# GpSimd's order of work inside an attention batch: the low halves of the weights move from the front to between the keys and the queries

## The reference

```python
x = x + tanh(g_xattn[0]) * attention(layernorm(x), ctx, ctx)   # 32 query heads, 8 key heads, D = 16, softmax over 128
x = x + tanh(g_ffn[0]) * ffn(layernorm(x))
# ffn: router logits over 7 experts, the 2 highest of each row, softmax over those two;
#      each expert and one shared expert: u = x Wup + b; g = silu(u Wgate + b) * u; g Wdown + b
#      result = sum over the two experts of prob * expert(x)  +  shared(x)
```

## Time and profile before

| | before |
|---|---|
| median of 3 runs | 1243.54 us (1243.29 to 1244.3) |
| the profiled execution's own time | 1242.8 us |
| its span, first to last instruction | 1240.7 us |
| TensorE busy over the span | 1154.8 us (93%) |
| VectorE busy | 818.6 us (66%) |
| ScalarE busy | 535.8 us (43%) |
| GpSimd busy | 388.8 us (31%) |
| the 32 `weights_lo` (L708), mean of one | 99.4 us, 3107 ns |
| mean granted TensorE clock | 0.982 of full speed |

### The profile page before, as it was taken

The page is one execution under the profiler, slowest core; times in us unless marked ns, Lnnn a source line. Parts: engine busy times, 40 slices in busy tenths (PEclk is TensorE's granted clock), DMA queues, the critical chain, the costliest instruction groups (busy, mean ns, idle before and its releaser), DMA issues.

```text
span 1240.7 us, 38694 instructions
## 1 busy us (share of the span) xinstructions
PE 1154.8 (93%) x14378; PEld 844.5 (68%) x14378; DVE 818.6 (66%) x1421; ACT 535.8 (43%) x1082; POOL 388.8 (31%) x454
## 2 busy tenths in 40 slices
PE   3878889999979999989899999999999999999998
PEld 2534444554456777778688887888888888877775
DVE  4888989999979689544444544544444444447898
ACT  2767779989889322122222222222222222222221
POOL 4465766666750000111111111111111110006762
PEclk9988999999979999999999999999999999999999
DMA  5675456565575253586644467435943346249985
GB/s 182 209 261 178 156 171 204 197 201 207 188 255 212 69 129 103 202 224 162 197 124 119 135 202 221 110 104 162 262 116 101 101 126 179 68 142 216 290 261 177
DMA packets 190496, 214.65 MB, mean 173 GB/s; under 512 B 115168, under 2 KB 115680, under 8 KB 190432
## 3 DMA queue, kind: packets, MB, share of 16 engines
q1 hardware_dynamic: 179712, 178.66, 47.9%
q0 software_dynamic: 10720, 35.14, 9.6%
HBM read 324.34 MB, written 64.49 MB: 313 GB/s over the span
## 4 chain that ended last, share of the span: by engine, by line
PE 51%; DVE 14%; SPq 12%; issue 9%; DMA 6%; POOL 3%; ACT 3%; DVEq 1%; ACTq 0%; POOLq 0%
PE PS L1675 29%; PE PS L1716 14%; DVE negm L1023 6%; SPq L459 3%; SPq L424 3%; PE PS L1496 3%; DMA bd<-in_bdown 2%; DMA qB<-negT 2%; PE PS L1530 2%; SPq L386 1%; SPq L420 1%; PE PS L1516 1%; ACT x2n L893 1%; POOL whl L708 1%; DVE xn L1009 1%
## 5 line engine op out<-in xcount | busy, mean ns | idle before, releaser
L1675 PE MATMUL PS<-uhl,wb 128*128 128x128 f16 (+1 forms) x4128 | 280.4, 229 | 8.5 <-DVE uhl L1277 7.9
L1675 PEld LDWEIGHTS PS<-uhl,wb 128*128 128x128 f16 x4128 | 264.9, 98 | 31.1 <-DVE uhl L1277 6.7
L1675 PE MATMUL PS<-xT,wb 128*128 128x128 f16 (+1 forms) x4128 | 279.8, 229 | 4.3 <-DVE gate L1164 1.6
L938 ACT ACTIVATE sl<-PS,bb 128x128 f32<-128x128 f32 (+1 forms) x344 | 106.9, 388 | 406.6 <-PE PS L1675 406.6
L1675 PEld LDWEIGHTS PS<-xT,wb 128*128 128x128 f16 x4128 | 264.0, 98 | 13.5 <-DVE gate L1164 1.7
L1716 PE MATMUL PS<-wb,ghl 128*128 128x512 f16 x1200 | 267.2, 379 | 1.2 <-DVE ghl L1289 1.2
L1716 PEld LDWEIGHTS PS<-wb,ghl 128*128 128x128 f16 x1200 | 115.9, 98 | 131.6 <-DVE ghl L1289 1.5
L928 ACT ACTIVATE u<-PS,bb 128x128 f32<-128x128 f32 (+1 forms) x344 | 106.8, 388 | 197.8 <-PE PS L1675 133.1
L759 POOL COPY ixr<-idx 128x2 int32 (+1 forms) x35 | 8.2, 233 | 549.1 <-DMA xT<-xs 406.7
L1023 DVE TENSOR_REDUCE negm<-PS 128x8 f16<-128x1024 f32 x128 | 155.2, 1212 | 26.2 <-PE PS L1496 25.5
L1284 DVE TENSOR_TENSOR g<-sl,u 128x512 f32<-128x512 f32 x102 | 70.5, 692 | 150.9 <-ACT sl L938 150.8
(11 more groups left out here) (159 smaller groups left out, 1201.4 us busy)
## 6 DMA issues: line engine op xcount, KB each, us to landing
wb<-wsc SPq DMA_DIRECT2D x219, 1024.0 KB
wst<-in_wall SPq DMA_DIRECT2D x32, 768.0 KB, 6.0
wsc<-whl SPq DMA_DIRECT2D x32, 768.0 KB, 4.4
ysl<-yb SPq DMA_DIRECT2D x43, 512.0 KB
bd<-in_bdown SPq DMA_DIRECT2D x74, 256.0 KB
X<-in_x SPq DMA_DIRECT2D x8, 1024.0 KB, 6.5
qB<-qT SPq DMA_DIRECT2D x32, 256.0 KB, 2.9
xnd<-xhl SPq DMA_DIRECT2D x32, 256.0 KB, 2.0
```

Of the source, the lines that this page charges most:

```text
L938: ins = act.activation(sl[:, m, ts], bank_of(PS[1], t, m, kind), ACT.Silu, bias=bb[:, par, bias_slot(kind, t), 1, m:m + 1], scale=1.0 / WS)
L1675: ins = pe.matmul(bank_of(bank, t, m, kind), wb[:, j, l, k, w, m * P:(m + 1) * P], rhs(x, k)[:, ts], start=(n == 0), stop=(n == len(TERMS) ...
```

## The change

In GpSimd's turn the call of `weights_lo` moves from the first place to the place between `split_k` and `split_q`. No operation is added, removed or resized, and no semaphore changes. The other four engines' programs are as they were.

```diff
                 after = follow(half, par, quad, 2)
                 later = follow(half, par, quad, 3)
-                if not start:
-                    weights_lo(*pv)
                 if after is not None:
                     values(*after)
                 if later is not None:
                     split_k(*later[:2])
+                if not start:
+                    weights_lo(*pv)
+                if later is not None:
                     split_q(*later[:2])
```

## The result

| | before | after |
|---|---|---|
| median, 22 runs of each | 1243.92 us (1238.57 to 1252.1) | 1248.28 us (1246.22 to 1252.11) |
| ratio to before | | 1.0031, 95% interval 1.0017 to 1.0045 |
| the profiled execution's own time, its span | 1242.8, 1240.7 us | 1246.86, 1244.8 us |
| mean granted TensorE clock | 0.982 | 0.971 |
| mean of the 32 `weights_lo` (L708) | 3107 ns | 3110 ns |

The change makes the kernel 0.31% slower, 3.9 us (0.0031 x 1243.92; the two medians as they stand differ by 4.4). The prediction was 1243.6 us with a range to 1246.6 and most of its chance on "no change": it was wrong. The changed kernel's lines lie one higher than before from the change on: L1467 is L1468, L1496 is L1497, L1009 is L1010, L1052 is L1053.

What follows compares the result with a forecast made beforehand. TensorE and VectorE were taken to bound attention's loop, with effects only in batches 1 to 12. Terms -0.44, -0.15 and +0.65 gave +0.06 us on 1242.8, 1242.9; plus 0.7 to the runs' median, 1243.6 us, range 1240.0 to 1246.6.

Steps and rivals of the forecast that it cites:

- What bounds the kernel; where the change acts: Attention: TensorE and VectorE busy some 47 of 50 us in the loop; effect only in batches 1 to 12, loop unchanged.
- What is late next: Even batches: VectorE's `xn` ends 0.64 us later, `qx` gets in before `wst`; `wst` and `maxes` come 1.51 us later.
- VectorE goes first: Rival, even batches: `wst` gets the ports before waiting `qx`, together -2.5 us, 1241.0 us; chance 0.17.
- The sum by batches, even turns: Start of `rec` in batches 6, 8, 10: -0.44, -0.15, +0.65 us; batch 2 gives 0; sum +0.06 us.
- The absorbed delays of batches 1, 4 and 12: Delays there taken as 0 behind DMA waits or late high halves; +2.0 us in the sum with their bounds.
- The sum by batches, odd turns: Batches 7, 9 and 11: no term of their own in the sum; the loop and the rest were put at 0.
- TensorE's idle time moves to the maxima products (L1496) behind them: Sign expected in the new profile if right: TensorE idles before these products, released by `maxes`; no cost given.
- where the granted clock is lost: Part of the unseen remainder, with where big transfers fall: both ways by 2 to 3 us; chance 0.10 together.
- The plain sum: Batches 6, 8, 10: three long `kx` waits, 4.9 us, gone; as rival at most 4.3 us, 1239.3 us; chance 0.05.

## Why the prediction was wrong

**What bounds the kernel; where the change acts.** Right. The new order in batches 6, 8 and 10 alone gives the whole loss, and the loop's 17 turns agree within 0.07 us in all six executions (157.07 to 157.14).

**What is late next.** Right, to 0.1 us. Forecast were `xn` later by 0.64 us and `wst` near 1.9 with `qx` near 1.3; measured were 1.81 us for `xn` (1.19 + 0.62) and 1.91 and 1.34. The rule that was named from the Trainium skill (SBUF — State Buffer, two separate sides), an exclusive lock for whoever starts first, fits every row shown here: `qx` started 0.25 us before `wst` and went first (154.10, 154.35), and with `Va` between them `wst` started first (149.86, 150.05) and `qx` paid. The rival "VectorE goes first" is thereby out for the changed kernel, and it is what the order with the keys first does.

**The sum by batches, even turns.** Forecast -0.44, -0.15, +0.65, together +0.06 us. The turns 6, 8 and 10 of the two first profiles differ by -0.48, -0.19 and +0.61, which is that forecast within 0.04; over three executions of either order the sum is +0.22. But the two gains are not what the prediction took them for. VectorE's idle time ahead of `rec` was 1.88 us in batch 6 and 1.60 in batch 8 because TensorE ran at half clock there, from 108.0 and from 132.0 us on; where the clock holds, it is 0.79, as in batch 10, and in the second profile of before it is 0.79 in batch 8 and 1.61 in batch 10. At full clock each of the three batches has the +0.65 of batch 10 (measured 0.6). The sum came out near zero because five of the nine even turns of the old order are made longer by the clock, which the prediction did not see: that is luck in part.

The absorbed delays of batches 1, 4 and 12 are not contradicted: the residual of batch 4 ends at 100.67 and 101.14 us after, at 99.34 to 101.60 in the four executions with the old order in those batches, and turn 12 takes 13.11 to 13.71 us in the new order, 13.08 to 13.50 in the old one. The scatter is too large to say more.

**The sum by batches, odd turns: the step that failed.** The sum stopped at the even batches. The prediction itself said that "TensorE's idle time moves to the maxima products (L1496) behind them" and gave this move no price, as if a wait cost only its length. It also left "where the granted clock is lost" to a chance of 0.10 "both ways", without asking in which turns the clock was lost already. It was one way, and it was most of the effect: the wait grew from 1.63 to 2.04 us and moved towards the turn's end, the clock fell to 0.50 behind it for mostly 7 us in place of 3.5, and turns 7, 9 and 11 lost 2.96 us in sum. With the even turns' 0.22 that is +3.2 us of the 3.9 measured (0.0031 x 1243.92), whose interval is 2.1 to 5.6. The rest is within what the runs can tell.

How firmly is the clock the cause? Shown: the fall stands in the records of the stretch that gets longer; work without use that fills the hole takes the loss away in two of three odd turns, and in the third the clock did fall; a `wst` that is not delayed takes it away in all three; another hole of 1.66 us brings part of it back. The means over all runs agree with this: the granted clock over the span is 0.973 for the change (22 runs), 0.975 with it in three even turns alone, 0.980 for before (35 runs), 0.983 with the added transposes and 0.984 with the keys first. Not shown: why the slow stretch is mostly 7 us long behind the new wait of 2.04 us and mostly 3.5 behind the old one of 1.63. The wait of 1.66 us for `Pt`, at the head of an odd turn, had 3.5 us each time, which speaks for the length of the wait; but the two also differ in what TensorE did on either side, and no run varies the length alone.

**The plain sum.** Rightly refused: VectorE was in the way. Only with `rstd1` moved as well, so that neither waits for the other, is there a gain of 0.5%, and then it owes nothing to the order.

## What to carry to other kernels

When a wait moves to another place on the engine that sets the time, give the new place a price of its own: compare the hole's length with others in the trace, look up the granted clock of the stretch behind each, and carry the sum through the next turn. Look up the clock of the rows that the sum starts from too: an idle time that a slow stretch made on another engine is not there in every execution. On GpSimd, the operation queued behind a long one matters more than the long one's own place, for it can get in between two operations of VectorE; a short copy there cost VectorE 0.1 us, a long one 1.0. And before reordering work inside a turn that is too long, ask what made it long: here a side task of 3 us stood ahead of it and could move into idle time.

## What the runs showed that was not expected

- A wait of some 2.04 us on TensorE was followed by a stretch at half clock in 9 of 9 cases, of about 7 us in seven: a turn of 9.9 us becomes 11.0. Waits of 1.62 to 1.66 us were followed by one in 7 of 9 cases in the order of before, in 3 of 3 with transposes behind the wait and in 3 of 3 with `wst` late, of about 3.5 us in all but one. The mean clock of a single run hardly tells: before is anywhere from 0.973 to 0.985 in the first series, after from 0.968 to 0.978.
- The same program's last three attention turns take 20.4 or 25.0 us, with the clock of the second of them at 1.00 or 0.50.
- `xn`, an operation of 0.53 us, held VectorE for 2.90 us behind GpSimd's `whl` in the kernel with `weights_lo` last; in the one with the new order and `rstd1` moved, VectorE's copy of `kT` ran beside `whl` in its usual 0.41 us (151.40 to 151.81 us, with `whl` from 151.32).
